# Layer 3 of a graph network with edges on partitions, more selected blocks, and another engine for one kind of transfer

## The chip, the cores and the metric

The kernel runs on one core of a Trainium2 chip. The metric is the time of one execution on the device in microseconds; the figure for a kernel is the median of several runs. A core has TensorE (matmuls and weight loads), VectorE, ScalarE, GpSimd and SyncE; the last three issue DMA transfers too.

## The reference

12,500 nodes with 32 features, 200,000 edges from a node `src` to a node `dst`, sorted by `dst`. Every edge gets a message from a four-layer network, the messages are averaged by `dst`, added to `x`, and each row is normalised.

```python
x_j, x_i = x[src], x[dst]
msg = concatenate([x_i, x_j - x_i], axis=-1)      # (200000, 64)
h = relu(msg @ W1 + b1)                           # 64
h = relu(h @ W2 + b2)                             # 128
h = relu(h @ W3 + b3)                             # 64
m = h @ W4 + b4                                   # 32
s   = segment_sum(m, dst, 12500)
cnt = segment_sum(ones, dst, 12500)
out = layernorm(x + s / maximum(cnt, 1)[:, None])
```

## The kernel before, in words

**Layer 1 is split.** `msg @ W1` is `x_j @ W1b + x_i @ (W1a - W1b)`. A prologue computes for every node the row `z_rows` (source part, f32) and the row `y_rows` (destination part, as three bf16 parts), and stores both in HBM. **Layer 4 is applied after the sum**, since it is linear: the main loop sums `h` of layer 3 and a column of ones by node, into `sums` (65 x 12,584 f32).

**Steps.** The edges are cut into S_N = 196 blocks of 1024 edges, one to a step. A block has two units (h = 0, 1) of 512 edges; a unit has four tiles of 128. The activations of layers 1 to 3 lie with features on partitions and 512 edges in the free dimension. There are two kinds of block:

- *Gathered* blocks (144 of them): GpSimd fetches the source rows with one indirect DMA for each 128 edges (L585, eight a block, 1147 in all, of which the first 40 read `x` itself), into a ring `xj` of R = 10 blocks. GpSimd waits for a ring slot until TensorE has transposed the block that was in it. TensorE turns the rows with four transposes (L919) straight into the PSUM bank of layer 1.
- *Selected* blocks (SB = 52, the first 53,248 edges, which the prologue sorts by source within each block): no gather. VectorE builds one-hots of the sources (L1377, eight chunks a block) and TensorE picks the rows with 113 small bf16 matmuls (L964). These are spread over the block's own step and the two before it (`PIECES`: chunks 0 to 2, then 3 to 5, then 6 and 7). ScalarE and VectorE copy the result (L698, L1386), and six bf16 matmuls apply layer 1 (L978).

`SORTED_AT` spreads the selected blocks evenly over the steps 7 to 188, at least three steps apart. The first AHEAD = 4 steps run in the prologue, between the stages of the sort; the rest is a loop whose number of passes is computed from the data (one pass here).

**One step s on TensorE**, in order: the source rows of s (L919, or the last piece of L964); the destination rows of s, a one-hot `pick` times a window of `y_rows` (L901); the transposes of layer 3 of block s-2 (L1004); the window sum of block s-3, 8 matmuls of `h3t` (128 edges x 65) with the one-hot of the destinations (L1019 gathered, L1016 selected); the pieces of L964 of the coming selected blocks; L978 if s is selected; layer 3 of s-1 (L996, two matmuls of 512 columns with w3s as weights, onto two halves of the partitions); layer 2 of s (L988, likewise on two halves of the rows).

**ScalarE** in step s: relu2 of s-1 (L724, two), copy_x, relu1 of s (L716), relu3 of s-1 (L731). **VectorE**: copy_x, copy_layer3 of s-2 (L1392, PSUM to `h3t`), `build_pick` of s+1 (L1366, L1367, L1369), `build_onehot` of s-2 (L1410, eight), `add_sums` of s-3 (L1425, one addition to `sums` for a selected block, two for a gathered one, with a register read of the window's place before each), then `build_hot` for selected blocks up to three steps on.

**SyncE** issues the block transfers, RX = 3 steps ahead: the dst list (`load_dst`, L458), the window of `y_rows` (`load_rows`, L468 or twice L473, each with a register read of its place), and the source windows of the selected blocks (L491). `load_rows` of s+3 waits until layer 1 of s has read its buffer.

**The tail.** After the last window sum: messages (L1082), transposes (L1092), the mean, the residual and the normalisation in chunks, and the stores.

Of the kernel before, what the change touches and what calls it, by code (L numbers as in the profile page):

```python
# [15 lines left out]
O = 32  # L16
# [15 lines left out]
SB = 52  # L32
# [81 lines left out]
def build(nc, x, src, dst, W1, b1, W2, b2, W3, b3, W4, b4, consts, bounds, out):  # L114
# [3 lines left out]
    with ctx:  # L118
# [44 lines left out]
        b3s = sb("b3s", [P, 1], F32)  # L163

# [56 lines left out]
        h3 = part(work, 8 * UE, (2, UE))  # L221
# [75 lines left out]
        s_l3, s_ht, s_agg = sem("layer3"), sem("layer3_turned"), sem("window_summed")  # L297
        s_h3a = sem("layer3_copied_by_scalar")
# [3 lines left out]
        s_r1, s_r3 = sem("relu1"), sem("relu3")  # L302
# [4 lines left out]
        s_open = sem("pass_open")  # L307
        s_begun = sem("gathers_begun")
# [74 lines left out]
        def _(sp):  # L383
# [34 lines left out]
            sp.dma_start(w3s[:, :], W3).then_inc(s_w, 16)  # L418
            sp.dma_start(b2s[:, :], b2.rearrange("(n a) -> n a", a=1)).then_inc(s_w, 16)
# [41 lines left out]
            def load_rows(s):  # L461
                u = s % RX
                if s >= RX:
                    for h in range(2):
                        sp.wait_ge(s_l1[h], s - RX + 1)
                if is_sorted(s):
                    first = sp.value_load(base_i[0:1, base_at(s, 0):base_at(s, 0) + 1], min_val=0, max_val=N)
                    sp.dma_start(ywin[:, u, :, :], y_rows[bass.ds(first, WIN), :, :].rearrange(  # L468
                        "(k n) c f -> (n c) k f", k=2)).then_inc(s_ywin[u], 16)
                else:  # L470
                    for h in range(2):
                        first = sp.value_load(base_i[0:1, base_at(s, h):base_at(s, h) + 1], min_val=0, max_val=N)
                        sp.dma_start(ywin[:, u, h, :], y_rows[bass.ds(first, KN), :, :].rearrange("n c f -> (n c) f"))\  # L473
                            .then_inc(s_ywin[u], 16)

# [18 lines left out]
            def load_first():  # L494
                for s in range(RX):
                    load_dst(s)
                    load_rows(s)

            def step(s):
# [4 lines left out]
                if s + RX < S_N:  # L504
                    load_dst(s + RX)
                    load_rows(s + RX)
# [11 lines left out]
            sp.wait_ge(s_ypad, 16)  # L518
            rows_stored(sp, s_yst)
# [110 lines left out]
        def _(act):  # L630
# [53 lines left out]
            act.wait_ge(s_w, 15 * 16)  # L684
            act.wait_ge(s_set, 2)

# [31 lines left out]
            def relu2(s):  # L718
                v = s % 2
                for h in range(2):  # L720
                    act.wait_ge(s_l2[h], s + 1)
                    if s >= 2:
                        act.wait_ge(s_l3, 2 * (s - 1))
                    nc.scalar.activation(h2[:, v, h, :], p_h2[:, h, :], ACT.Relu, bias=b2s[:, 0:1]).then_inc(s_r2[h], 1)  # L724

            def relu3(s):
                v = s % 2
                act.wait_ge(s_l3, 2 * (s + 1))
                if s >= 2:
                    act.wait_ge(s_ht, s - 1)  # L730
                nc.scalar.activation(h3[:, v, :], p_h3, ACT.Relu, bias=b3s[:, 0:1]).then_inc(s_r3, 1)  # L731

            def copy_layer3(s):
                act.wait_ge(s_ht, s + 1)
                if s >= 2:
                    act.wait_ge(s_agg, s - 1)
                nc.scalar.activation(h3t[:, s % 2, :, :, 0:H3], p_ht.rearrange("p (t h f) -> p t h f", t=UT, h=2), ACT.Copy)\
                    .then_inc(s_h3a, 1)

            def step(s):  # L740
# [826 lines left out]
```

## Time and profile before

| | |
|---|---|
| median of 3 runs | 1571.46 us (1568.09 to 1571.53) |
| span of the profiled execution | 2441.1 us (no other time of it is given) |
| TensorE matmuls / weight loads busy | 1767.5 us (72%) / 1040.0 us (43%) |
| VectorE busy | 947.9 us (39%) |
| ScalarE busy | 602.6 us (25%) |
| GpSimd busy | 1125.9 us (46%) |
| mean granted TensorE clock | 0.764 of 2.4 GHz |

The profiled execution took 870 us longer than the median run. A share of its span is therefore not a share of an ordinary run: it has to be asked of each stretch whether it looks as it would without the profiler. "Releaser" in the views is what ended an idle time; "issue" means that nothing which the profile shows did.

### The profile page before, as it was taken

Reading aid. Unit: us, or ns where it says so; the run is one execution under the profiler, and the core shown is the slowest. Engines: PE = TensorE matmul, PEld = TensorE weight load, DVE = VectorE, ACT = ScalarE, POOL = GpSimd, SP = SyncE. Lnnn points to the kernel's source line nnn. Section 1 sums busy time; section 2 is a strip of 40 time slices with the busy share of each in tenths; the row PEclk is TensorE's granted clock in tenths of the full one; section 3 lists DMA queues with packets and bytes.
Section 4 is the critical chain, followed back from the end, with each engine's and each line's share of the span. In section 5 each row is a group of like instructions: output and inputs, shape, how many; then the busy total and the mean of one; then the engine's idle time right before and its main releaser. Section 6 shows DMA issues by size and latency. Waiting matters only on the chain.

```text
span 2441.1 us, 39243 instructions
## 1 busy us (share of the span) xinstructions
PE 1767.5 (72%) x13131; PEld 1040.0 (43%) x13131; DVE 947.9 (39%) x3086; ACT 602.6 (25%) x945; POOL 1125.9 (46%) x1165
## 2 busy tenths in 40 slices
PE   3133777777768777878787778786867778777797
PEld 2112444444444444444444444444444444444454
DVE  3663343333333343333333333443333333333356
ACT  2233122222212222212222222222221222122234
POOL 5275444453544454354545454544444454444411
PEclk7555787877878787777778877777877877787888
DMA  5334643343434443353434353544344344444332
GB/s 128 98 93 88 200 112 112 106 140 94 136 101 116 126 121 109 103 147 91 135 105 136 104 152 92 152 109 114 104 123 115 111 114 109 133 118 118 109 106 59
DMA packets 189929, 283.06 MB, mean 116 GB/s; under 512 B 84614, under 2 KB 90169, under 8 KB 189156
## 3 DMA queue, kind: packets, MB, share of 16 engines
q1 hardware_dynamic: 152341, 241.67, 33.7%
q0 software_dynamic: 36704, 37.00, 7.3%
q10 hardware_dynamic: 682, 1.85, 0.3%
q8 instruction: 108, 1.77, 0.3%
q14 instruction: 94, 0.77, 0.1%
HBM read 266.51 MB, written 13.73 MB: 115 GB/s over the span
## 4 chain that ended last, share of the span: by engine, by line
PE 63%; issue 23%; another core or an unknown queue 6%; DVE 3%; ACT 2%; DMA 1%; SPq 1%; DVEq 0%; POOL 0%; ACTq 0%; POOLq 0%
PE ps L964 22%; PE ps L996 12%; PE ps L988 10%; PE ps L1019 5%; PE ps L1004 4%; PE ps L919 3%; PE ps L901 3%; PE ps L1016 2%; PE ps L978 2%; ACT work L716 1%; ACT work L731 1%; DMA sums<-in_src 1%; DVE region L1410 0%; DVE region L1292 0%
## 5 line engine op out<-in xcount | busy, mean ns | idle before, releaser
L585 POOL DMA_INDIRECT xj<-z_rows,src_t x1107 | 1074.5, 971 | 1190.9 <-PE ps L919 787.7
L964 PE MATMUL ps<-region,x_p 128*96 128x150 bf16 (+53 forms) x5876 | 569.6, 243 | 416.6 <-issue 407.2
L964 PEld LDWEIGHTS ps<-region,x_p 128*96 128x96 bf16 x5876 | 440.6, 142 | 572.9 <-issue 566.7
L731 ACT ACTIVATE work<-ps,b3s 128x512 f32<-128x512 f32 x196 | 134.7, 687 | 1335.5 <-PE ps L996 1037.1
L996 PE MATMUL ps<-work,w3s 128*64 128x512 f32 x784 | 356.6, 840 | 21.2 <-issue 21.1
L1377 DVE TENSOR_SCALAR region<-region,cst 128x1565 bf16<-128x1565 int16 (+6 forms) x416 | 245.7, 634 | 268.0 <-remote 256.3
L988 PE MATMUL ps<-work,w2s 64*128 64x512 f32 x784 | 298.1, 827 | 6.8 <-ACT work L716 5.6
L724 ACT ACTIVATE work<-ps,b2s 128x512 f32<-128x512 f32 x392 | 250.7, 684 | 161.0 <-PE ps L988 82.7
L1392 DVE COPY work<-ps 128x512 f32<-128x512 f32 x194 | 133.4, 687 | 336.4 <-PE ps L1004 217.0
L1386 DVE CAST work<-ps 96x512 bf16<-96x512 f32 x52 | 35.7, 686 | 513.9 <-PE ps L964 506.8
L1410 DVE TENSOR_SCALAR region<-iota_g,dst_rel 128x42 f32<-128x42 f32 x1120 | 185.7, 250 | 0.0
L716 ACT ACTIVATE work<-ps,b1s 128x512 f32<-128x512 f32 x196 | 134.8, 688 | 199.9 <-PE ps L901 155.0
L988 PEld LDWEIGHTS ps<-work,w2s 64*128 64x128 f32 x784 | 81.7, 240 | 237.5 <-issue 184.7
L1425 DVE TENSOR_TENSOR sums<-sums,ps 65x42 f32 (+1 forms) x340 | 67.8, 199 | 273.0 <-remote 109.5
L1019 PE MATMUL ps<-region,work 128*65 128x42 f32 x2304 | 168.8, 238 | 5.6 <-DVE sums L1425 3.6
L1019 PEld LDWEIGHTS ps<-region,work 128*65 128x65 f32 x2304 | 166.6, 148 | 8.3 <-issue 8.0
L1004 PE MATMUL ps<-cst,work 128*128 128x128 f32 x784 | 132.9, 294 | 50.1 <-ACT work L731 44.0
L919 PEld LDWEIGHTS ps<-cst,xj 128*128 128x128 f32 x576 | 65.7, 150 | 146.6 <-issue 146.5
L996 PEld LDWEIGHTS ps<-work,w3s 128*64 128x64 f32 x784 | 74.2, 166 | 118.6 <-issue 102.0
L1004 PEld LDWEIGHTS ps<-cst,work 128*128 128x128 f32 x784 | 86.4, 146 | 87.8 <-ACT work L731 54.1
L919 PE MATMUL ps<-cst,xj 128*128 128x128 f32 x576 | 102.1, 304 | 14.3 <-DVE work L1333 14.3
L901 PE MATMUL ps<-region,ywin 126*64 126x512 bf16 x496 | 92.9, 406 | 12.1 <-remote 12.1
(156 smaller groups left out, 826.3 us busy)
## 6 DMA issues: line engine op xcount, KB each, us to landing
dstb<-dst_rows SPq DMA_DIRECT2D x196, 252.0 KB
region<-src_rows SPq DMA_DIRECT2D x104, 391.2 KB
region<-src_rows SPq DMA_DIRECT2D x52, 407.2 KB
region<-src_rows SPq DMA_DIRECT2D x52, 403.2 KB
region<-src_rows SPq DMA_DIRECT2D x52, 376.2 KB
region<-src_rows SPq DMA_DIRECT2D x52, 375.8 KB
region<-src_rows SPq DMA_DIRECT2D x52, 374.0 KB
region<-src_rows SPq DMA_DIRECT2D x52, 366.2 KB
```

The costliest lines, as they stand in the source:

```text
L585: pool.indirect_dma_start(out=xj[:, u, j % UT, j // UT, 0:w], out_offset=None, in_=rows, in_offset=bass.IndirectOffsetOnAxis(ap=cols[:, j: ...
L716: nc.scalar.activation(h1[:, v, :], p_h1, ACT.Relu, bias=b1s[:, 0:1]).then_inc(s_r1, 1)
L724: nc.scalar.activation(h2[:, v, h, :], p_h2[:, h, :], ACT.Relu, bias=b2s[:, 0:1]).then_inc(s_r2[h], 1)
L901: added = nc.tensor.matmul(p_h1[h * H1:(h + 1) * H1, :], rows, pick[:, v, k, h * UE:(h + 1) * UE], start=False, stop=k == steps - 1, skip_ ...
L919: turned = nc.tensor.matmul(to[:, t * T:(t + 1) * T], xj[:, u, t, :, :].rearrange("p h f -> p (h f)"), ident, start=t == 0, stop=True, is_ ...
L964: chosen = nc.tensor.matmul(ps[0:XP, XBANK[h], lo - h * UE:hi - h * UE], xb[:, a, :], hot[:, q % QN, at + lo:at + hi], start=not begun[h], ...
L988: nc.tensor.matmul(p_h2[:, h, :], w2s[r:r + H1, :], h1[r:r + H1, s % 2, :], start=True, stop=True).then_inc(s_l2[h], 1)
L996: nc.tensor.matmul(p_h3[h * H3:(h + 1) * H3, :], w3s[:, :], h2[:, s % 2, h, :], start=True, stop=True).then_inc(s_l3, 1)
L1004: turned = nc.tensor.transpose(p_ht[:, t * T:(t + 1) * T], h3[:, s % 2, t * T:(t + 1) * T], ident)
L1019: summed = nc.tensor.matmul(p_agg[:, h * KN:(h + 1) * KN], h3t[:, v, t, h, :], onehot[:, v, j, 0:KN], start=t == 0, stop=t == UT - 1)
L1377: nc.vector.tensor_scalar(hot[:, q % QN, 0:CW[c]], spread[:, q % QE, 0:CW[c]], cst[:, C_PID:C_PID + 1], None, ALU.is_equal).then_inc(s_hot, 1)
L1410: last = nc.vector.tensor_scalar(onehot[:, v, j, 0:w], nodes[:, :], dst_rel[:, n * PT + j:n * PT + j + 1], None, ALU.is_equal)
```

## The change

Three edits in one:

1. **Layer 3 with edges on partitions.** The activations h2 of 128 edges become the stationary operand and w3s (128 x 64) the moving one, so that the result has edges on partitions, as the window sum needs it. The four transposes, ScalarE's relu3 and the buffer h3 go. The bias can't be a per-partition scalar now: VectorE takes max(h @ W3, -b3) with a row `floor3` that holds -b3, and the missing b3 is added behind the sum, as a bias b3 @ W4 folded into the last row of w4s. The window sum comes one step earlier (block s-2 in step s), layer 3 has two PSUM banks, and the loop has one step fewer at its end. In VectorE's step the copy and `add_sums` stand first, and `build_onehot` is of s-1.
2. **SB = 60.** 60 blocks are selected and 136 gathered, in 1083 indirect DMAs in place of 1147. The selected ones stand three steps apart in 55 of 59 cases, four in the others; before it was 23 of 51.
3. **`load_rows` on ScalarE**, behind relu1 of the step, in place of SyncE. In the prologue ScalarE issues the first three blocks' rows before its step 0.

```diff
-SB = 52
+SB = 60
...
-        p_x, p_h1, p_h3 = ps[:, 0, :], ps[:, 1, :], ps[:, 4, :]
+        p_x, p_h1 = ps[:, 0, :], ps[:, 1, :]
...
-        p_ht = ps[:, 5, :]
+        p_h3 = ps[:, 4:6, :].rearrange("p v (t h f) -> p v t h f", t=UT, h=2)
+        p_b4 = ps[H3:H3 + 1, 7, 256:256 + O]
...
         def layer3_copied(eng, s):
-            if s < AHEAD - 2:
-                eng.wait_ge(s_h3a, s + 1)
-            else:
-                eng.wait_ge(s_h3c, s + 3 - AHEAD)
+            eng.wait_ge(s_h3c, s + 1)
...
+            sp.dma_start(floor3[:, :], b3.unsqueeze(0).to_broadcast([P, H3])).then_inc(s_w, 16)
...
+            act.wait_ge(s_base, 1)
+            act.wait_ge(s_ypad, 16)
+            rows_stored(act, s_yst)
+            load_first_rows()
...
                 if s < S_N:
                     relu1(s)
-                if 2 <= s < AHEAD:
-                    copy_layer3(s - 2)
-                if s >= 1:
-                    relu3(s - 1)
+                if s + RX < S_N:
+                    load_rows(s + RX)
...
             def layer3(s):
-                if s >= 1:
-                    pe.wait_ge(s_r3, s)
+                if s >= 2:
+                    layer3_copied(pe, s - 2)
                 for h in range(2):
                     pe.wait_ge(s_r2[h], s + 1)
-                    nc.tensor.matmul(p_h3[h * H3:(h + 1) * H3, :], w3s[:, :], h2[:, s % 2, h, :],
-                                     start=True, stop=True).then_inc(s_l3, 1)
-            def turn_layer3(s):
-                pe.wait_ge(s_r3, s + 1)
-                if s >= 1:
-                    layer3_copied(pe, s - 1)
-                for t in range(UT):
-                    turned = nc.tensor.transpose(p_ht[:, t * T:(t + 1) * T], h3[:, s % 2, t * T:(t + 1) * T], ident)
-                turned.then_inc(s_ht, 1)
+                    for t in range(UT):
+                        made = nc.tensor.matmul(p_h3[:, s % 2, t, h, :], h2[:, s % 2, h, t * T:(t + 1) * T], w3s[:, :],
+                                                start=True, stop=True)
+                made.then_inc(s_l3, 1)
...
-                stay_busy({S_N + 1: 3}.get(s, 0))
-                if 2 <= s <= S_N + 1:
-                    turn_layer3(s - 2)
-                stay_busy({S_N: 4, S_N + 1: 2, S_N + 2: 8}.get(s, 0))
-                if s >= 3:
-                    sum_window(s - 3)
+                stay_busy({S_N: 4, S_N + 1: 6}.get(s, 0))
+                if s >= 2:
+                    sum_window(s - 2)
...
+            pe.wait_ge(s_w, 16 * 16)
+            nc.tensor.matmul(p_b4, b3s[0:H3, :], w4s[0:H3, :], start=True, stop=True).then_inc(s_b4, 1)
...
+            def last_weights():
+                dve.wait_ge(s_b4, 1)
+                link(nc.vector.tensor_tensor(w4s[H3:H3 + 1, :], w4s[H3:H3 + 1, :], p_b4, ALU.add))
...
             def copy_layer3(s):
-                dve.wait_ge(s_ht, s + 1)
+                dve.wait_ge(s_l3, s + 1)
...
-                nc.vector.tensor_copy(h3t[:, s % 2, :, :, 0:H3], p_ht.rearrange("p (t h f) -> p t h f", t=UT, h=2))\
+                nc.vector.tensor_tensor(h3t[:, s % 2, :, :, 0:H3], p_h3[:, s % 2, :, :, :],
+                                        floor3[:, :].unsqueeze(1).unsqueeze(1).to_broadcast([P, UT, 2, H3]), ALU.max)\
                     .then_inc(s_h3c, 1)
...
             def step(s):
+                if 2 <= s <= S_N + 1:
+                    copy_layer3(s - 2)
+                if s >= 3:
+                    add_sums(s - 3)
                 if s < S_N and is_sorted(s):
                     copy_x(s)
-                if AHEAD <= s <= S_N + 1:
-                    copy_layer3(s - 2)
                 if s + 1 < S_N:
                     build_pick(s + 1)
-                if 2 <= s <= S_N + 1:
-                    build_onehot(s - 2)
-                if s >= 3:
-                    add_sums(s - 3)
+                if 1 <= s <= S_N:
+                    build_onehot(s - 1)
```

## Rows read from the trace of the kernel before

**Rows 1.** The page, its first line.
```profile
span 2441.1 us, 39243 instructions
```

**Rows 2.** The waits: who waited for whom, us in total, times, longest.
```profile
POOL xj L585 <- PE ps L919: 787.7, 101, 14.0
PEld ps L964 <- issue: 566.7, 725, 3.1
```

**Rows 3.** Timeline of TensorE while gathers run: start, us, engine, line, operation, count.
```profile
1006.89 1.71 PE L964 MATMUL ps<-region,x_p 128*96 128x155 bf16 x31
1008.99 0.30 PE L964 MATMUL ps<-region,x_p 128*96 128x148 bf16 x2 [0.40 <-issue]
```

**Rows 4.** Timeline of TensorE after the last gather.
```profile
2353.76 1.09 PE L1019 MATMUL ps<-region,work 128*65 128x42 f32 x16
2354.67 2.41 PE L964 MATMUL ps<-region,x_p 128*96 128x26 bf16 x39
...
2361.66 2.69 PE L964 MATMUL ps<-region,x_p 128*96 128x155 bf16 x45
...
2372.59 0.66 PE L919 MATMUL ps<-cst,xj 128*128 128x128 f32 x4
...
2373.51 0.66 PE L1004 MATMUL ps<-cst,work 128*128 128x128 f32 x4
...
2376.03 1.13 PE L988 MATMUL ps<-work,w2s 64*128 64x512 f32 x4
2377.09 0.66 PE L919 MATMUL ps<-cst,xj 128*128 128x128 f32 x4
```

**Rows 5.** GpSimd: its group of gathers in the page, and four of its timeline.
```profile
L585 POOL DMA_INDIRECT xj<-z_rows,src_t x1107 | 1074.5, 971 | 1190.9 <-PE ps L919 787.7
...
115.66 1.06 POOL L585 DMA_INDIRECT xj<-z_rows,src_t  x1 [43.15 <-DMA z_rows<-work]
...
205.44 0.94 POOL L585 DMA_INDIRECT xj<-z_rows,src_t  x1 [14.89 <-issue]
206.69 0.94 POOL L585 DMA_INDIRECT xj<-z_rows,src_t  x1 [0.30 <-issue]
...
2336.93 0.94 POOL L585 DMA_INDIRECT xj<-z_rows,src_t  x1 [0.30 <-issue]
```

**Rows 6.** Three steps, busy us of PE, PEld, DVE, ACT, POOL; granted clock, DMA.
```profile
2352.34:2372.59 20.25, 20.25 (x221) 13.95 (x220) 13.15 (x46) 8.17 (x13) 0.00 (x0) 1.00 0.13 36
```

**Rows 7.** Weight loads: timeline, and by line (duration ns min/median/max).
```profile
2351.28 0.30 PEld L988 LDWEIGHTS ps<-work,w2s 64*128 64x128 f32 x4 [0.81 <-issue]
...
2353.26 0.42 PEld L1004 LDWEIGHTS ps<-cst,work 128*128 128x128 f32 x4 [0.23 <-issue]
...
L1004 PEld LDWEIGHTS ps<-cst,work x784: 137/141/231, 157.0 to 2411.2; 128*128 128x128 f32 x196
...
L988 PEld LDWEIGHTS ps<-work,w2s x784: 182/187/336, 128.0 to 2404.7; 64*128 64x128 f32 x196
```

**Rows 8.** VectorE's copy and second addition, and SyncE's loads of a gathered block's rows.
```profile
2349.45 0.69 DVE L1392 COPY work<-ps 128x512 f32<-128x512 f32 x1 [2.08 <-PE ps L1004]
...
2352.60 0.20 DVE L1425 TENSOR_TENSOR sums<-sums,ps 65x42 f32 x1 [0.75 <-DVE sums L1425]
...
2354.32 1.69 SPq L473 DMA_DIRECT2D ywin<-y_rows  x2
```

**Rows 9.** The loop's start (VectorE, TensorE), the last step's start, the last window sum.
```profile
206.66 6.81 DVE L1350 TENSOR_SCALAR region<-src,blk 52x26 int16<-52x26 int16 x41
...
230.09 0.26 DVE L1350 TENSOR_SCALAR region<-src,blk 52x155 int16<-52x155 int16 x1 [1.13 <-issue]
...
255.12 0.66 PE L919 MATMUL ps<-cst,xj 128*128 128x128 f32 x4
...
2400.11 0.66 PE L919 MATMUL ps<-cst,xj 128*128 128x128 f32 x4
...
2414.97 1.11 PE L1019 MATMUL ps<-region,work 128*65 128x42 f32 x16 [0.30 <-DVE sums L1425]
```

More of the change, by code:

```diff
@@ L163, in build @@
         b3s = sb("b3s", [P, 1], F32)
+        floor3 = sb("floor3", [P, H3], F32)
         ring_at = 4 * PT * WIN + 4 * PE2
@@ L220, in build @@
         x16 = part(work[:, :].bitcast(BF16), 12 * UE, (2, UE))
-        h3 = part(work, 8 * UE, (2, UE))
         h3t = part(work, 10 * UE, (2, PT * (H3 + 1))).rearrange("p v (t h f) -> p v t h f", t=UT, h=2)
@@ L301, in build @@
         s_moved, s_centre = sem("windows_moved"), sem("centring_chain")
-        s_r1, s_r3 = sem("relu1"), sem("relu3")
+        s_r1 = sem("relu1")
         s_r2 = [sem(f"relu2_unit{n}") for n in range(2)]
@@ L307, in build @@
         s_open = sem("pass_open")
+        s_b4 = sem("bias_through_w4")
         s_begun = sem("gathers_begun")
@@ L459, in load_dst @@
                     .then_inc(s_dwin[u], 16)
[L461 to L474, printed above, removed]
             def store_windows(c):
@@ L496, in load_first @@
                     load_dst(s)
-                    load_rows(s)
             def step(s):
@@ L683, in _, with load_rows, load_first_rows @@
                 split_more(g)
-            act.wait_ge(s_w, 15 * 16)
+            act.wait_ge(s_w, 16 * 16)
             act.wait_ge(s_set, 2)
+            def load_rows(s):
+                u = s % RX
+                if s >= RX:
+                    for h in range(2):
+                        act.wait_ge(s_l1[h], s - RX + 1)
+                if is_sorted(s):
+                    first = act.value_load(base_i[0:1, base_at(s, 0):base_at(s, 0) + 1], min_val=0, max_val=N)
+                    act.dma_start(ywin[:, u, :, :], y_rows[bass.ds(first, WIN), :, :].rearrange(
+                        "(k n) c f -> (n c) k f", k=2)).then_inc(s_ywin[u], 16)
+                else:
+                    for h in range(2):
+                        first = act.value_load(base_i[0:1, base_at(s, h):base_at(s, h) + 1], min_val=0, max_val=N)
+                        act.dma_start(ywin[:, u, h, :], y_rows[bass.ds(first, KN), :, :].rearrange("n c f -> (n c) f"))\
+                            .then_inc(s_ywin[u], 16)
+            def load_first_rows():
+                for s in range(RX):
+                    load_rows(s)
+            act.wait_ge(s_base, 1)
+            act.wait_ge(s_ypad, 16)
+            rows_stored(act, s_yst)
+            load_first_rows()
             def window_sources(c):
@@ L722, in relu2 @@
                     if s >= 2:
-                        act.wait_ge(s_l3, 2 * (s - 1))
+                        act.wait_ge(s_l3, s - 1)
                     nc.scalar.activation(h2[:, v, h, :], p_h2[:, h, :], ACT.Relu, bias=b2s[:, 0:1]).then_inc(s_r2[h], 1)
[L726 to L738, printed above, removed]
             def step(s):
@@ L783, in _ @@
                     act.sem_inc(s_begun, 1)
+                    act.wait_ge(s_tables, 1)
+                    load_first_rows()
                     for s in range(AHEAD):
@@ L1064, in _ @@
                 turn_masked()
-                for s in range(AHEAD, S_N + 3):
+                for s in range(AHEAD, S_N + 2):
                     step(s)
@@ L1179, in weights @@
             def weights():
-                dve.wait_ge(s_w, 15 * 16)
+                dve.wait_ge(s_w, 16 * 16)
                 w = w1par[0:XP, :]
@@ L1464, in _ @@
             count_passes()
+            last_weights()
             dve.wait_ge(s_end, 1)
```

11 lines of the change are left out of this document (5 added, 6 removed).

## The prediction

> **What bounds the kernel now.** I read the page first, then the waits, TensorE's timeline with gathers running and without, GpSimd's rows, and last the weight loads. The profiled execution has a span of 2441.1 us and the median run takes 1571.46, so the profile slowed this kernel by 870 us [rows 1]; no other time of that execution is given, so its span is its own time. The sum can't be made on that span; I first rebuild the median from stretches that show no stall.
>
> The reader should see where the 870 us lie. TensorE's weight loads waited 566.7 us before the small matmuls of L964 to "issue", that is to nothing the program asked for [rows 2]. The timeline shows the form: 31 matmuls of L964 in 1.71 us, then one or two every 0.7 us [rows 3]. Once GpSimd's last gather has started at 2336.93, the same line runs 39 matmuls in 2.41 us and 45 in 2.69 without a gap, at a granted clock of 1.00, the 2.4 GHz level [rows 4, 5, 6]. I take the dribble for a cost of profiling and price TensorE from the clean stretch [rows 4]: a gathered step runs from L919 to L919, 2372.59 to 2377.09, 4.50 us. Two gathered steps and one selected take 2352.34 to 2372.59, 20.25 us with TensorE busy for all of it [rows 6], so a selected step is 20.25 - 9.0 = 11.25.
>
> Two accounts of the median follow. TensorE: step 6 starts at 255.12 and step 195 at 2400.11, the end of the span is 41 us later [rows 9]. Before step 6 VectorE's 59 copies of L1350 ran at 6.81 us for 41, to 213.5, and then dribbled too, the other 18 until 230.4; at the first pace those take 3.0 us, so I start at 255 - 14 = 241 [rows 9]. 241 + 137 x 4.50 + 52 x 11.25 + 41 = 1484. GpSimd: gathers from z_rows begin at 115.66, and there are 1107 of them; undisturbed ones start 1.25 us apart, and the mean is 0.971 busy + 0.30 = 1.27; the wait for the pass count costs 14.6 more than such a gap; after the last gather comes at least the last step with its tail, 41 [rows 5, 9]. That gives 115.7 + 1107 x 1.25 to 1.27 + 14.6 + 41 = 1555 to 1577. The median lies inside this second account and 87 us above the first. So unprofiled the gathers set the pace, though in the profiled execution GpSimd waited 787.7 us for TensorE [rows 2]: there it was TensorE that was held up.
>
> **The change part by part.**
>
> *60 blocks instead of 52.* 64 of 1147 gathers go: 64 x 1.27 = 81 us off GpSimd. TensorE swaps 8 gathered for 8 selected steps: 8 x (11.25 - 4.50) = +54 us. VectorE gets 8 x 8 source one-hots of about 0.6 us and is busy 13.15 of the 20.25 us of three steps now [rows 6], so this hides. Selected steps stand 3 apart nearly everywhere (55 of 59 distances; before 23 of 51).
>
> *Layer 3, removed.* Four transposes (L1004), the window sum (L1019) and both 512-column matmuls of L996 take from 2373.51 to L988 at 2376.03 in a gathered step: 2.52 us, of which the sum comes back in another place [rows 4]. ScalarE's relu of 0.69 us goes too; it is not on the path, since ScalarE is busy 8.17 of 20.25 [rows 6].
>
> *Layer 3, added.* Eight matmuls with 128 edges as the stationary side and 64 moving columns. An f32 matmul leaves two records (16 for the eight of L1019 [rows 4]), so that is 16 weight loads of 128 f32 columns. No row shows a full-height one in a dense stream; the bounds come from its neighbours. Low: L1019 loads 65 columns and reaches the next line 0.91 us later, 57 ns a record [rows 4]. Next: the transposes of L1004 load 128 columns, but four in 0.42 us with 0.14 each, so (0.42 - 0.14) / 3 = 94 ns [rows 7]. Nearest: L988 loads 128 f32 columns per row half, two at once; four take 0.30 and each 0.187, so the second pair follows after 0.11 us [rows 7]. High: load and stream not overlapped, L988's 0.107 and a stream like L1019's whole record of 0.057, 0.16. I take the load's own time, 0.107, and the 2 ns that a stream adds where it never stops (L1019's 57 against 54, two cycles for each of 65 columns at 2.4 GHz, the rate that also makes 107 out of 128): 0.109 us. 16 x 0.109 = 1.75, plus 0.91 for the window sum (its value when a full-width line follows) and 0.10 for the change to L988's half tiles, as now before it. 2.76 against 2.52: +0.24 us per step, although fewer columns are streamed. 189 steps: +45 us.
>
> The rule that speaks against this change is in the Trainium skill, TensorE: Matmul & The Clock Gate, section LDWEIGHTS: a load takes its columns divided by 1.2 ns, whatever the rows. It gives 107 ns for 128 columns and the trace's 0.11 us agrees; for 96 columns of bf16 it gives 80, and L964's 39 matmuls in 2.41 us (62 ns each, loads included) [rows 4] disagree. By the page alone layer 3 is 16 x 107 = 1.71 us; by the rows 1.75.
>
> *Waits inside the step.* VectorE now copies layer 3 of s-2 first in step s, as a maximum from the same bank; L1392 took 0.69 [rows 8], and the maximum has the same 512 columns, so 0.69 (no row shows its two-operand form). Then it adds the sums: two additions, 0.94 us start to start [rows 8]. Layer 3 of s-2 ends 1.06 us before TensorE's step s begins, and the copy starts about 0.15 later, so the copy ends at -0.2 and the second addition at +0.9. TensorE wants both at +0.92 (L919 to L1004, 2372.59 to 2373.51 [rows 4]). No stall while VectorE is on time. In a selected step it also has copy_x, pick, one-hot and three source one-hots ahead of the next copy: by these rows it ends about 0.3 us late, 60 x 0.25 = 15 us at most. I take 7.
>
> *ScalarE issues the dst rows.* Two loads with their register reads took SyncE 1.69 us a gathered step [rows 8]. ScalarE goes from 0.69 x 4 to 0.69 x 3 + 1.69 = 3.8 us in a step of 4.74. They are issued behind relu1, for buffers that layer 1 of the same step has just freed, so they wait for nothing; queued behind them is relu2, which waits for L988 anyway, ending at about +4.9 when they are over at +3.8. Cost 0. Without that cover it is up to 1.1 us a step. SyncE's queue loses the loads and keeps its dst lists and windows; GpSimd's is untouched. In the prologue six loads (5 us) stand before step 0, beside the sort on VectorE: I take 0, with 5 as the bound.
>
> *Rest.* The bias matmul and five tiny operations of VectorE before the loop: +1.5 us. One step fewer at the end saves a window sum of 1.11 and the additions behind it, 0.94: -2 [rows 8, 9].
>
> **The sum.** TensorE: 241 + 129 x 4.74 + 60 x 11.49 + 41 + 1.5 - 2 = 1582, + 7 for VectorE = 1589. GpSimd: 1571 - 81 = 1490. The longer decides: the bound moves from the gathers to TensorE, and 1589 is 1.1% above the median. About 0.3% (5 us) is what a measurement here can tell from no change.
>
> **Rivals.** Each ns of the load pace is worth 189 x 16 = 3.0 us. No change (1566 to 1576) lies at 101 to 105 ns.
>
> 1. *The loads are cheaper, and the gathers stay the bound* (the other side). If full-height loads follow each other as L1019's do, TensorE needs 1589 - 3.0 x 52 = 1433, and GpSimd's 1490 decides; at the transposes' 94 ns it is 1589 - 45 = 1544. The point from which it is faster: under 101 ns. For it: both paces stand in the trace. Against it: the first has half the columns, the other transposed data; L988's second pair waited the full 0.11.
> The same page of the Trainium skill (Back-to-back issue gap) gives 81 ns for a sustained pair of load and 128-column matmul. Here that would be 1589 - 84 = 1505, by a stream that hides the load better than L988 shows; L964's 62 ns are below it, for bf16.
>
> 2. *TensorE was the bound already*, with 87 us of stalls that the clean stretch doesn't show, some of the "issue" being real. Then nothing comes back from the gathers: 1571 + 54 + 45 - 1 = 1669. For it: the stalls in [rows 3]. Against it: the gather account meets the median with no free term.
>
> 3. *VectorE or ScalarE gets late*, as copies and additions now stand at the head of VectorE's step: 0.2 to 0.3 us on each of 189 steps, 1625 to 1645.
>
> 4. *The change does not do what it says*: what it takes from the gathers and what it lays on TensorE cancel, 1566 to 1576; at 101 to 105 ns.
>
> **How the numbers follow.** Forecast (TensorE bound, 1576 to 1615) 0.40; rival 1 0.30 (0.20 near 1490 to 1505, 0.10 at 1520 to 1560); rival 2 0.13; rival 3 0.07; rival 4 0.10. Faster 0.30, same 0.10, slower 0.60. The likeliest case's own range is 1576 to 1615. From 1490 to 1645 leaves out rival 2 and a few in a hundred of the low end; both signs lie in it.
>
> **What would show it.** In the clean stretch after the last gather: 16 loads of layer 3 in about 1.8 us (at 0.9 rival 1, at 2.6 no overlap); a gathered step of about 4.7; L1019 or L1016 without a wait on VectorE; relu2 starting just behind L988 (else ScalarE's issues delay it). GpSimd's undisturbed pace still 1.25, with 1083 gathers. The prediction is wrong if that step is under 4.5 us, or if the median sits on GpSimd's account, near 1490.

## The result and the profile after

The changed kernel takes 1607.61 us (median of 4 runs, 1604.63 to 1611.45) against 1569.83 for the kernel before on the same chip: a ratio of 1.0251, 95% interval 1.0224 to 1.0278. It is slower by more than twice what was forecast (1589 us, +1.2% on this median). Its profiled execution was one of these runs (1604.63 us, span 1602.7), so this profile, unlike the one of before, can be read as an ordinary run.

The page of the changed kernel: the span; the chain of work that ended last, by line; then two groups (count | busy us, mean ns | idle before).

```profile
span 1602.7 us, 43751 instructions
...
POOL xj L565 73%; DMA sums<-in_src 1%; PE ps L987 0%; PE ps L1003 0%; PE ps L1065 0%; DVE region L1280 0%; DVE region L1279 0%; DVE work L1140 0%; DMA xj<-z_rows,src_t 0%; PE ps L840 0%; DMA z_rows<-work 0%; DVE work L1146 0%; PE ps L1075 0%; PE ps L978 0%; POOL region L597 0%
...
L565 POOL DMA_INDIRECT xj<-z_rows,src_t x1043 | 1162.4, 1114 | 317.9 <-issue 317.3
```

The chain is gathers for 73% of the span: GpSimd is still the bound. 1043 gathers from z_rows (1107 before, [rows 5]) take 1114 ns each, plus 0.305 idle (317.9 / 1043): 1.419 us start to start, where the prediction had 1.27. Undisturbed ones are as short as ever, 0.94 us. The two timelines show where the rest lies, first GpSimd's, then VectorE's.

```profile
299.64 0.94 POOL L565 DMA_INDIRECT xj<-z_rows,src_t  x1 [0.30 <-issue]
300.89 0.95 POOL L565 DMA_INDIRECT xj<-z_rows,src_t  x1 [0.30 <-issue]
302.14 2.83 POOL L565 DMA_INDIRECT xj<-z_rows,src_t  x1 [0.30 <-issue]
305.28 0.95 POOL L565 DMA_INDIRECT xj<-z_rows,src_t  x1 [0.30 <-issue]
...
1019.75 0.94 POOL L565 DMA_INDIRECT xj<-z_rows,src_t  x1 [0.30 <-issue]
1020.99 0.95 POOL L565 DMA_INDIRECT xj<-z_rows,src_t  x1 [0.30 <-issue]
1556.64 0.94 POOL L565 DMA_INDIRECT xj<-z_rows,src_t  x1 [0.30 <-issue]
```

```profile
301.27 1.29 DVE L1401 TENSOR_SCALAR region<-iota_g,dst_rel 128x42 f32<-128x42 f32 x8
302.48 1.69 DVE L1365 TENSOR_SCALAR region<-region,cst 128x1629 bf16<-128x1629 int16 x3
304.29 0.69 DVE L1382 TENSOR_TENSOR work<-ps,floor 128x512 f32<-128x512 f32 x1
...
1019.95 1.67 DVE L1365 TENSOR_SCALAR region<-region,cst 128x1565 bf16<-128x1565 int16 x3
```

The gather of 302.14 lasts 2.83 us, and VectorE builds three source one-hots (L1365) under it, from 302.48 to 304.17; it ends 0.80 us behind them. Yet the row of three that begins at 1019.95 costs nothing. From 280 to 1500 us the gathers last 157 us more than 0.944 each would make, and all but 12 of these 157 lie on gathers that overlap such one-hots. A row of three that begins 0.32 to 0.34 us behind a gather's start holds it up for 1.87 to 1.89 us (31 rows, 58 us together), one that begins 0.20 or 0.21 behind it for none (41 rows).

TensorE, two gathered steps and one selected in the middle of the run, and its transposes near the end:

```profile
1010.35 1.71 PE L954 MATMUL ps<-region,x_p 128*96 128x144 bf16 x29
...
1017.21 0.66 PE L909 MATMUL ps<-cst,xj 128*128 128x128 f32 x4
1017.80 0.41 PE L891 MATMUL ps<-region,ywin 126*64 126x512 bf16 x2
1018.34 1.11 PE L1003 MATMUL ps<-region,work 128*65 128x42 f32 x16
1019.28 2.41 PE L954 MATMUL ps<-region,x_p 128*96 128x26 bf16 x39
1021.53 1.94 PE L987 MATMUL ps<-w3s,work 128*128 128x64 f32 x16
1023.40 1.13 PE L978 MATMUL ps<-work,w2s 64*128 64x512 f32 x4
...
1032.22 0.99 PE L954 MATMUL ps<-region,x_p 128*96 128x144 bf16 x13
...
1521.07 1.09 PE L909 MATMUL ps<-cst,xj 128*128 128x128 f32 x4 [5.89 <-DMA xj<-z_rows,src_t]
```

It runs nearly without a gap until about 1500 us, three steps in 21.87 us (1010.35 to 1032.22), and waits for gathers only in the last blocks: 5.89, 1.33, 5.89 and 1.10 us, 14.2 together. Until then it lives on the blocks that GpSimd had fetched ahead. Behind the second of the long waits the granted clock is 0.50 (1545 to 1557 us), the lower of its two levels (1.2 GHz), and the sixteen matmuls of L987 take 3.66 us in place of 1.98, so that the waits cost more than the 14.2. So two accounts end close to each other again, GpSimd's at 1603 and TensorE's some 20 us below.

### The profile page after: what moved, and what is told of

Read it like the earlier page. It is cut to its first block, busy times and chain, and to the rows that moved or that the text cites. A ratio compares the mean times of both kernels' runs of the same rounds, so it can differ in the third digit from the quotient of the medians.

```text
span 1602.7 us, 43751 instructions
## 1 busy us (share of the span) xinstructions
PE 1456.2 (91%) x15630; PEld 1161.9 (72%) x15630; DVE 993.4 (62%) x3162; ACT 468.7 (29%) x755; POOL 1219.8 (76%) x1101
## 4 chain that ended last, share of the span: by engine, by line
POOL 73%; issue 20%; PE 2%; DVE 2%; DMA 1%; ACT 0%; DVEq 0%; SPq 0%; POOLq 0%; ACTq 0%
POOL xj L565 73%; DMA sums<-in_src 1%; PE ps L987 0%; PE ps L1003 0%; PE ps L1065 0%; DVE region L1280 0%; DVE region L1279 0%; DVE work L1140 0%; DMA xj<-z_rows,src_t 0%; PE ps L840 0%; DMA z_rows<-work 0%; DVE work L1146 0%; PE ps L1075 0%; PE ps L978 0%; POOL region L597 0%
## 5 line engine op out<-in xcount | busy, mean ns | idle before, releaser
L565 POOL DMA_INDIRECT xj<-z_rows,src_t x1043 | 1162.4, 1114 | 317.9 <-issue 317.3
L954 PEld LDWEIGHTS ps<-region,x_p 128*96 128x96 bf16 x6780 | 389.2, 124 | 45.5 <-issue 45.5
L954 PE MATMUL ps<-region,x_p 128*96 128x127 bf16 (+54 forms) x6780 | 409.5, 218 | 0.0
L987 PE MATMUL ps<-w3s,work 128*128 128x64 f32 x3136 | 394.6, 280 | 0.0
L987 PEld LDWEIGHTS ps<-w3s,work 128*128 128x128 f32 x3136 | 375.9, 196 | 25.1 <-issue 25.1
L1382 DVE TENSOR_TENSOR work<-ps,floor 128x512 f32<-128x512 f32 x196 | 135.4, 691 | 320.8 <-PE ps L987 316.4
L1365 DVE TENSOR_SCALAR region<-region,cst 128x1629 bf16<-128x1629 int16 x480 | 272.3, 617 | 8.4 <-DMA region<-src_rows 7.3
L978 PE MATMUL ps<-work,w2s 64*128 64x512 f32 x784 | 227.9, 659 | 0.9 <-ACT work L720 0.9
L1003 PE MATMUL ps<-region,work 128*65 128x42 f32 x2176 | 157.3, 236 | 23.8 <-DVE sums L1416 9.4
L1003 PEld LDWEIGHTS ps<-region,work 128*65 128x65 f32 x2176 | 144.4, 143 | 45.4 <-issue 37.7
L1000 PEld LDWEIGHTS ps<-region,work 128*65 128x65 f32 x960 | 73.5, 139 | 28.0 <-issue 28.0
L1000 PE MATMUL ps<-region,work 128*65 128x84 f32 x960 | 81.9, 239 | 11.8 <-DVE sums L1416 6.0
L1401 DVE TENSOR_SCALAR region<-iota_s,dst_rel 128x84 f32<-128x84 f32 x480 | 89.7, 277 | 0.0
```

Of the source, the lines that this page charges most:

```text
L565: pool.indirect_dma_start(out=xj[:, u, j % UT, j // UT, 0:w], out_offset=None, in_=rows, in_offset=bass.IndirectOffsetOnAxis(ap=cols[:, j: ...
L954: chosen = nc.tensor.matmul(ps[0:XP, XBANK[h], lo - h * UE:hi - h * UE], xb[:, a, :], hot[:, q % QN, at + lo:at + hi], start=not begun[h], ...
L978: nc.tensor.matmul(p_h2[:, h, :], w2s[r:r + H1, :], h1[r:r + H1, s % 2, :], start=True, stop=True).then_inc(s_l2[h], 1)
L987: made = nc.tensor.matmul(p_h3[:, s % 2, t, h, :], h2[:, s % 2, h, t * T:(t + 1) * T], w3s[:, :], start=True, stop=True)
L1000: summed = nc.tensor.matmul(p_agg, h3t[:, v, t, h, :], onehot[:, v, j, :], start=j == 0, stop=j == PT - 1)
L1003: summed = nc.tensor.matmul(p_agg[:, h * KN:(h + 1) * KN], h3t[:, v, t, h, :], onehot[:, v, j, 0:KN], start=t == 0, stop=t == UT - 1)
```

## The experiments

Two theories and a third. **G**: GpSimd's gathers set the end in both kernels, and VectorE's one-hots hold gathers up, more in the changed one. **T**: TensorE sets the end of the changed kernel; long gathers are a by-product. **D**: transfers or their queues stretch the gathers. "Ratio" is to the kernel before, with the 95% interval.

### One part at a time

**e1**, loads of the dst rows on ScalarE, all else as before. 

> The kernel before with edit 3 alone: ScalarE issues the dst rows. Theory G (GpSimd's gathers set the pace in both kernels; in the changed one VectorE's work stretches a gather from 1.25 to 1.41 us start to start): no change, 1565 to 1575 us, and a gather at its old mean. Rival D (the loads on ScalarE's queue are what stretches the gathers): 0.14 us on each of 1107 gathers, 1600 us or more. Rival T (TensorE is what the changed kernel waits for): no change. If the profile of this one is not slowed by the profiler, it also shows which engine the old schedule waits for.

**e2**, `SB = 60` in place of 52, all else as before. 

> The kernel before with edit 2 alone: SB = 60. Theory G: 64 gathers fewer take 80 us off GpSimd, the stretch of 8 more selected blocks gives 10 to 25 back, and TensorE's account of 1484 + 54 = 1538 is close: 1530 to 1550 us. Rival T in its strong form (TensorE was the bound already, rival 2 of the prediction): 1571 + 54 = 1625. Rival D: as G.

**e3**, the new layer 3 and VectorE's new order, all else as before. 

> The kernel before with edit 1 alone: the new layer 3 with VectorE's new order, SB = 52, loads on SyncE. Theory G, with the stretch as a result of VectorE's new order: about 3 us for each of 52 selected blocks where it was 1, so 1107 gathers at 1.39 us, 1660 to 1680 us. Rival T: TensorE 1484 + 45 = 1529, hidden under the gathers: 1565 to 1580. If the stretch is there in the old order too, also 1565 to 1580.

**e4**, the changed kernel with the old layer 3. 

> The changed kernel with its edit 1 undone (old layer 3, SB = 60, loads on ScalarE). Theory G: as SB = 60 alone, 1530 to 1550 us. Rival D: 1600 or more. Rival T: TensorE's 1538, so 1535 to 1545, and then layer 3 is worth 60 to 70 us in the changed kernel instead of the 45 of the prediction.

Measured: e1 1568.31 us, ratio 1.0004 (0.9994 to 1.0014); e2 1566.38, 0.9993 (0.9977 to 1.0010); e3 1632.87, 1.0432 (1.0408 to 1.0456); e4 1554.08, 0.9911 (0.9894 to 0.9928). The loads are free in the kernel before, as forecast. With SB = 60 they are worth 12 us: e2 and e4 differ in them alone. Eight more selected blocks alone are worth nothing, where G had expected 20 to 40 us. The new layer 3 costs 65 us alone and 53 in the full change. Only e1 fell into G's range; e3 lies 27 us below it and e4 4 us above, so G's direction held and the size of the hold-up was not forecast. The groups of gathers in the four pages, in this order:

```profile
L566 POOL DMA_INDIRECT xj<-z_rows,src_t x1107 | 1106.0, 999 | 337.5 <-issue 336.2
```

```profile
L585 POOL DMA_INDIRECT xj<-z_rows,src_t x1043 | 1126.0, 1080 | 317.9 <-issue 317.0
```

```profile
L584 POOL DMA_INDIRECT xj<-z_rows,src_t x1107 | 1162.8, 1050 | 337.5 <-issue 335.6
```

```profile
L566 POOL DMA_INDIRECT xj<-z_rows,src_t x1043 | 1110.2, 1064 | 317.9 <-issue 317.0
```

Same instruction, same program on GpSimd, and its mean runs from 999 to 1114 ns. In none of them does GpSimd wait for TensorE for longer than the 0.3 us that it pauses anyway. So its account can be written down: e1's span of 1565.9 us less 1107 x (0.999 + 0.305) = 1443.5 leaves 122 for what lies ahead of the first gather (78) and behind the last (44). With 122 + gathers x (mean + 0.305):

| kernel | gathers | mean us | account | span |
|---|---|---|---|---|
| e2, SB = 60 | 1043 | 1.080 | 1567 | 1565.7 |
| e3, new layer 3 | 1107 | 1.050 | 1622 | 1626.6 |
| e4, old layer 3, SB = 60 | 1043 | 1.064 | 1550 | 1552.3 |
| the change | 1043 | 1.114 | 1602 | 1602.7 |

All four spans are met within 5 us. Each mean is that of the same profile, so the account shows that the time follows the gathers' length, and not why that differs. In e2 the 64 gathers that go save 83 us, and 0.081 us on each of the other 1043 takes 84 back; a row of three one-hots costs 0.14 us in e1 and 0.82 in e2 (280 to 1500 us). D falls with e1 and e4: the loads on ScalarE's queue make no gather longer (1.064 us in e4, 1.080 in e2 with the loads on SyncE). The other transfers are tested by e5. T is not refuted by these, since TensorE's account is close too.

### The one-hots taken away

**e5** cuts every source one-hot to 64 columns, in the changed kernel; **e6** does so in e3, **e16** in the kernel before.

```diff
-                nc.vector.tensor_scalar(hot[:, q % QN, 0:CW[c]], spread[:, q % QE, 0:CW[c]], cst[:, C_PID:C_PID + 1], None,
+                if q < QN:
+                    nc.vector.memset(hot[:, q, :], 0.0).then_inc(s_hot, 1)
+                    return
+                w = 64
+                nc.vector.tensor_scalar(hot[:, q % QN, 0:w], spread[:, q % QE, 0:w], cst[:, C_PID:C_PID + 1], None,
```

> The changed kernel, but each of VectorE's source one-hots (480, 0.62 us each) covers 64 columns in place of up to 1629; the first five are set to zero instead. So the rows of the selected blocks are wrong. Semaphores, transfers and TensorE's work are those of the changed kernel. Theory G (the gathers set the end, and they are long because VectorE's one-hots hold them up): every gather at 0.94 us busy, 1.25 start to start; GpSimd's account falls to 78 + 1043 x 1.25 + 14 + 45 = 1441 us, and the time to TensorE's own account, 1575 to 1590 us; GpSimd then waits for TensorE in the profile. Rival T (TensorE sets 1607 and long gathers are a by-product): 1603 to 1611. Rival D (transfers stretch the gathers): gathers stay at 1.41 us, 1603 to 1611.

> The same shortening of the one-hots in the kernel with the new layer 3 alone (SB = 52, loads on SyncE, 1632.9 us as it is). Theory G: gathers at 1.25 us, GpSimd's account 123 + 1107 x 1.25 = 1507 us, TensorE's by the prediction 1529: 1525 to 1540 us, about 100 less. Rival T (layer 3 is dear on TensorE itself, some 60 us): 1615 to 1633. Rival D: 1630.

> The kernel before with the source one-hots cut to 64 columns (the rows of the selected blocks are wrong; TensorE's work, transfers and semaphores stay). Theory G: the gathers pay 0.035 us less each than the 0.999 of the kernel with loads on ScalarE, 123 + 1107 x 1.265 = 1523, TensorE's 1484 below it: 1515 to 1530 us. If TensorE had been the bound before (rival 2 of the prediction): 1560 to 1570.

Measured: e5 1581.09 us, ratio 1.0107 (1.0085 to 1.0129); e6 1533.58, 0.9805 (0.9780 to 0.9831); e16 1527.78, 0.9749 (0.9724 to 0.9775). All three lie inside G's ranges, 27, 99 and 41 us below the same kernels with full one-hots. From e5's page, and its waits (engine and line waited for: us, times, longest):

```profile
L565 POOL DMA_INDIRECT xj<-z_rows,src_t x1043 | 1002.8, 961 | 394.1 <-issue 303.9
...
POOL xj L565 <- PE ps L909: 90.3, 46, 2.6
```

The gathers are back at 0.961 us, and now GpSimd waits for TensorE, 90.3 us in 46 places, which it never did in the changed kernel. TensorE did the same matmuls in both, at the same pace: three steps take 21.89 us in e5 (1001.31 to 1023.20). T had 1603 to 1611 and falls. D falls altogether, since the transfers are the same. Layer 2 of step 188 and of step 195 show where the time goes, in the changed kernel and then in e5:

```profile
1509.03 1.13 PE L978 MATMUL ps<-work,w2s 64*128 64x512 f32 x4
...
1569.28 1.13 PE L978 MATMUL ps<-work,w2s 64*128 64x512 f32 x4
```

```profile
1506.90 1.13 PE L978 MATMUL ps<-work,w2s 64*128 64x512 f32 x4
...
1544.36 1.13 PE L978 MATMUL ps<-work,w2s 64*128 64x512 f32 x4
```

Up to step 188 TensorE is 2 us apart in the two; the last seven steps take 60.2 us in the one and 37.5 in the other, since in the changed kernel they wait for gathers and then run at a lower clock. Nor is it VectorE's lateness: TensorE waits 9.4 and 6.0 us for `add_sums` in the changed kernel (L1003, L1000) and 12.3 and 4.5 in e5.

The runs also split the price of the new layer 3 at SB = 52: with the one-hots cut it costs 6 us (e6 less e16), with them whole 65 (e3). So some 59 of the 65 are hold-ups.

e16's mean is 0.963 with 1107 gathers: 122 + 1107 x 1.268 = 1526, its span 1525.8. So before the change, too, GpSimd was the bound.

### The same one-hots in another order

**e7**, the changed kernel, and **e8**, the old layer 3 with SB = 56: one-hots one at a time between VectorE's other work.

```diff
+                todo = [(STEPS[s + lead], c) for lead in (1, 2, 3) if s >= AHEAD and s + lead < S_N and is_sorted(s + lead)
+                        for c in PIECES[3 - lead]]
...
                 if s >= 3:
                     add_sums(s - 3)
+                if todo:
+                    build_hot(*todo.pop(0))
...
                 if s + 1 < S_N:
                     build_pick(s + 1)
+                if todo:
+                    build_hot(*todo.pop(0))
```

> The changed kernel with the same work in another order on VectorE: the two or three source one-hots of a step no longer stand in a row at its end (1.7 us together), but one behind add_sums, one behind build_pick, the rest behind build_onehot. Theory G: one of 0.6 us can hold a gather up for less than a row of three (up to 1.9 us): stretch of a gather from 0.17 to 0.05 to 0.10 us on the mean, and the time to 1580 to 1590, TensorE's account. Rival T: 1603 to 1611, or more, since VectorE's copies and picks come later. If the stretch goes by the total of one-hot time and not by how it lies, no change in it.

> Old layer 3, SB = 56, loads on ScalarE, the source one-hots spread: one behind build_pick, one behind build_onehot, the rest behind add_sums. Theory G: TensorE's account 1484 + 4 x 6.75 = 1511; GpSimd's 123 + 1075 x 1.25 = 1467 plus a stretch of 0.03 to 0.08 us a gather, 1500 to 1553; so 1511 to 1550, best of all so far. Rival T: about 1540 to 1560, between the kernel before and the one with SB = 60.

Measured: e7 1580.86 us, ratio 1.0101 (1.0078 to 1.0123), as e5; e8 1608.30, 1.0277 (1.0255 to 1.0299), where G had 1511 to 1550. The gathers of e7, then e8:

```profile
L565 POOL DMA_INDIRECT xj<-z_rows,src_t x1043 | 1068.1, 1024 | 330.8 <-issue 311.4
```

```profile
L566 POOL DMA_INDIRECT xj<-z_rows,src_t x1075 | 1164.2, 1083 | 327.7 <-issue 326.8
```

With e7 TensorE is the bound again, and G's range of 1580 to 1590 is met. e8 still meets the account (122 + 1075 x 1.388 = 1614, span 1615.6), so GpSimd's price is right and only the size of the hold-up was guessed wrong. One at a time, a one-hot of 0.63 us costs 0.16 us in e7 and 0.31 in e8 (from 280 to 1500 us). Spreading them is no remedy that can be relied on: the cost goes by where they fall in the gather's 1.25 us, and that changes with every schedule.

### The mode of the one-hot

The Trainium skill has two rules that bear on this. SBUF — State Buffer, Who interferes with whom: GpSimd reaches SBUF through VectorE's second pair of ports, and a VectorE instruction in a mode that uses both pairs, if it comes first, blocks GpSimd, descriptor writing included, until it is over. Vector Engine (DVE) Microarchitecture Reference, Performance modes: a one-source instruction on 16-bit data takes the four-a-cycle mode only if the outermost dimensions of input and output are both even, or equal; otherwise it runs at two a cycle on one pair. No run here sees a port; what follows tests the rule's consequence.

**e9** to **e11** gave the output rows. 

> The changed kernel with each source one-hot written to an output of 3, 5, 7 or 11 rows (same addresses, same values; the chunk of 1613 columns gets two columns more) while the input stays one run. The Trainium skill (Vector Engine (DVE) Microarchitecture Reference, Performance modes) says that a one-source instruction then leaves the four-wide mode that holds both port pairs and runs at two elements a cycle on one pair; SBUF - State Buffer says that only the two-pair modes hold GpSimd up. Theory G with this mechanism: a one-hot takes about 0.9 us in place of 0.62, the gathers stay at 0.94 us all the same, and the time falls to TensorE's 1580 to 1590 although VectorE works 130 us more. Rival: the hold-up comes from VectorE's long instructions whatever their mode: gathers as long as before or longer, 1600 to 1640 us. If the one-hot stays at 0.62 us, the shape did nothing and the run says nothing.

> Old layer 3, SB = 60, loads on ScalarE (1554 us), with the one-hots written in rows. Theory G: GpSimd's account 123 + 1043 x 1.25 = 1427, TensorE's 1484 + 54 = 1538: 1535 to 1545 us. Rival (mode does not matter): 1555 to 1600.

> The same with SB = 54, where the two accounts meet: GpSimd 123 + 1091 x 1.25 = 1487, TensorE 1484 + 2 x 6.75 = 1498. Theory G: 1495 to 1510 us, 4% under the kernel before. Rival (mode does not matter): 1555 to 1600.

Measured: e9 1611.41 us, ratio 1.0273 (1.0236 to 1.0310); e10 1550.23, 0.9895 (0.9865 to 0.9924); e11 1561.29, 0.9971 (0.9955 to 0.9987). In e9's page the one-hot still takes 616 ns:

```profile
L1369 DVE TENSOR_SCALAR region<-region,cst 128x1629 bf16<-128x1629 int16 x480 | 271.9, 616 | 8.4 <-DMA region<-src_rows 7.3
```

Rows without a gap are one run in memory, and were probably merged back to one; that is not shown, since a view gives only the number of columns. The expectation had said that a one-hot of 0.62 us would make the run say nothing, and so it is: G's three ranges are missed, and these runs say nothing on the mode. e9 and e10 repeat the changed kernel and e4. e11 is a point at SB = 54, with the account at 122 + 1091 x 1.317 = 1559 and the span 1558.3:

```profile
L568 POOL DMA_INDIRECT xj<-z_rows,src_t x1091 | 1104.6, 1012 | 332.6 <-issue 330.5
```

**e12** (the changed kernel) and **e13**, **e15** (old layer 3, loads on ScalarE, SB = 54 and 56) put a column of padding between the rows of the input, written so by the transfer:

```diff
+CX = [w + -w % 3 for w in CW[:-1]] + CW[-1:]
+ROWS = [3] * (CN - 1) + [5]
...
+        def padded(q, c):
+            r, w = ROWS[c], CX[c] // ROWS[c]
+            return spread[:, q % QE, 0:r * (w + 1)].rearrange("p (r w) -> p r w", r=r)[:, :, 0:w]
...
-                nc.vector.tensor_scalar(hot[:, q % QN, 0:CW[c]], spread[:, q % QE, 0:CW[c]], cst[:, C_PID:C_PID + 1], None,
+                to = hot[:, q % QN, 0:CX[c]].rearrange("p (r w) -> p r w", r=ROWS[c])
+                nc.vector.tensor_scalar(to, padded(q, c), cst[:, C_PID:C_PID + 1], None,
```

> The changed kernel, with the source windows written by their transfer as 3 (the last chunk 5) rows with one column of padding between them, so that the input of a one-hot really has three rows where its output is one run; same values, up to two columns more. Theory G with the mechanism of the Trainium skill (Vector Engine (DVE) Microarchitecture Reference, Performance modes; SBUF - State Buffer, Who interferes with whom): the one-hot goes from 0.62 to about 0.9 us and no longer holds GpSimd: gathers at 0.94 to 0.97 us, time 1578 to 1590 us, TensorE's account. Rival (long instructions hold the gathers up in any mode): gathers 1.12 us or more, 1607 to 1640 us. If the three times as many packets of the windows make them late, VectorE or TensorE waits for them and the time rises above 1590 with short gathers.

> Old layer 3, SB = 54, loads on ScalarE, windows in padded rows. Theory G: GpSimd 123 + 1091 x 1.25 = 1487, TensorE 1484 + 13.5 = 1498: 1495 to 1512 us. Rival: gathers stay at 1.01 us or more, 1555 to 1570.

Measured: e13 1510.25 us, ratio 0.9640 (0.9607 to 0.9673), inside G's range; e12 1626.08, 1.0380 (1.0344 to 1.0416), outside all but the last clause. From e12's page and waits:

```profile
L573 POOL DMA_INDIRECT xj<-z_rows,src_t x1043 | 1004.8, 963 | 436.3 <-issue 302.1
...
L1375 DVE TENSOR_SCALAR region<-region,cst 128x1629 bf16<-128x1629 int16 x480 | 459.4, 1006 | 7.8 <-DMA region<-src_rows 7.5
...
POOL xj L573 <- PE ps L917: 134.2, 52, 3.2
...
PE ps L1011 <- DVE sums L1426: 58.6, 64, 4.4
```

From e13's timelines, three one-hots and the gathers across them:

```profile
1003.89 2.86 DVE L1396 TENSOR_SCALAR region<-region,cst 128x1566 bf16<-128x1566 int16 x3
...
1002.83 0.95 POOL L574 DMA_INDIRECT xj<-z_rows,src_t  x1 [0.30 <-issue]
1004.08 0.94 POOL L574 DMA_INDIRECT xj<-z_rows,src_t  x1 [0.30 <-issue]
1005.32 0.94 POOL L574 DMA_INDIRECT xj<-z_rows,src_t  x1 [0.30 <-issue]
1006.57 0.94 POOL L574 DMA_INDIRECT xj<-z_rows,src_t  x1 [0.31 <-issue]
```

The one-hots are 60% longer, and no gather is held up by them: of 98 rows of three in e13 between 280 and 1500 us not one adds 0.1 us. The run beside it is e11, with the same split and no padding: gathers of 1.012 us against 0.966, 1561.29 us against 1510.25. That settles length against form: what holds a gather is the fast form of the one-hot, not VectorE's being busy, as the two pages say. GpSimd is still the bound in e13 (122 + 1091 x 1.271 = 1509, the span 1509.4), where G had put TensorE; its account at 1.25 us a gather was too low.

e12 is slow for another reason, the last line of its waits: after 2.86 us of one-hots VectorE comes late to `add_sums`, which now stands at the head of its step, and TensorE waits 58.6 us in 64 places. **e14** spreads the one-hots as e7 does, on top of the padding. 

> The changed kernel with padded windows (1626 us, gathers 0.96, one-hots 1.01 us) and, besides, the one-hots of a step spread: one behind add_sums, one behind build_pick, the rest behind build_onehot. Theory V (the 1626 come from VectorE being late with add_sums after a row of three one-hots of 2.86 us: TensorE waited 0.9 us for it once per selected block): the wait goes, 1578 to 1590 us, TensorE's account. Rival (the three times as many packets of the windows slow TensorE's or VectorE's data): 1615 to 1630.

Measured: 1585.43 us, ratio 1.0119 (1.0093 to 1.0145), inside theory V's range: 41 us of e12's excess were that lateness, and the packets are not at fault.

**e15** moves the balance. 

> Old layer 3, padded windows, loads on ScalarE, SB = 56 in place of 54. GpSimd's account 123 + 1075 x 1.271 = 1489, TensorE's 1484 + 27 = 1511: 1508 to 1520 us, TensorE the bound. If the clean stretch made TensorE's account too long, 1495 to 1505.

Measured: 1501.03 us, ratio 0.9587 (0.9561 to 0.9614), the fastest of all and 4.1% under the kernel before. That is below the 1508 to 1520 expected and in the range of the second case. GpSimd's account is 122 + 1075 x 1.270 = 1487 and the span 1498.3, and the chain that ended last is 79% TensorE, so TensorE is the bound; its forecast of 1511 was 10 too long.

```profile
PE 79%; DVE 5%; issue 5%; ACTq 4%; DMA 4%; ACT 2%; SPq 0%; POOL 0%; DVEq 0%; POOLq 0%
```

## Why the prediction was wrong

The direction was right and the size was not: +2.5% where +1.2% was forecast. The time lies in the range of the likeliest case, 1576 to 1615, by luck: that case had TensorE as the bound and GpSimd at 1490, and it was GpSimd, at 1602. One of the prediction's own signs of being wrong came, a time that sits on GpSimd's account, though not near 1490.

- **GpSimd is the bound before the change.** Right (e16). Its account of 1555 to 1577 came out, but by offsetting terms: gathers begin at 78, not 115.7 us; the 14.6 us of waiting for the pass count isn't on GpSimd in e1's profile; and a gather costs 1.304 from start to start, not 1.25 to 1.27 (e1, whose time is that of the kernel before). The slowed profile had fewer hold-ups than an ordinary run.
- **"GpSimd: 1571 - 81 = 1490", at a pace "still 1.25".** This is the step that failed. Of the undisturbed gather the 1.25 is right. The mean rose from 1.304 to 1.419: the 64 gathers that go save 83 us, and 0.115 on each of the other 1043 costs 120. So 122 + 1043 x 1.419 is 1602. The prediction priced VectorE's source one-hots as VectorE's time only, "so this hides", and never asked what they do to GpSimd; no rival had it. A sign stood in its own rows: a gather of 0.971 us on the mean beside an undisturbed one of 0.94 [rows 5]. In that trace the gathers last 29 us more than 0.944 each would make, and 20 of these lie on gathers that overlap the one-hots.
- **"The bound moves from the gathers to TensorE."** Wrong by 20 us. Without hold-ups it does (e5, e7: GpSimd waits).
- **TensorE: 1582, with 7 for VectorE 1589.** e5 measured 1581 (span 1577.7). The sum is nearly right by terms that cancel. The loop begins earlier than taken: step 6 at 181 us, not 242.5. Three steps take 21.87, not 20.97. The three-step base was itself 20.90, not 20.25 (e4, first part of layer 1 to the next, below), with 0.61 us of idle time before it that the stretch behind the last gather doesn't show.

```profile
1008.06 0.84 PE L987 MATMUL ps<-work,w1p 96*64 96x512 bf16 x6 [0.61 <-issue]
1028.96 0.84 PE L987 MATMUL ps<-work,w1p 96*64 96x512 bf16 x6 [0.63 <-issue]
```

- **Layer 3: +0.24 us per step, +45.** Measured (21.87 - 20.90) / 3 = +0.32 (between e4 and the changed kernel). The sixteen loads take 1.87 us (1021.53 to 1023.40), 0.117 each, not 1.75; none of the lower prices that the prediction weighed came out. (Its 94 ns for the transposes is 93 by its own rows; nothing hangs on it.) Besides, 0.54 us pass from the dst rows to the window sum (1017.80 to 1018.34) where 0.34 was the old distance: the second addition ends at 1018.20, 0.99 after the step's start, not +0.9, and the sum starts 0.14 later. It is late by 0.2 in two steps of three, 24 us, where 7 were taken.
- **Rest, +1.5 us.** Too low by about 9: in the prologue TensorE now waits 7.21 us for VectorE's copy of layer 3, and VectorE begins the 59 copies of the sort's end at 148.09 us instead of 138.37 (e4). In the changed kernel it hid behind the gathers.
- **ScalarE's loads, 0.** Right at SB = 52 (e1); at SB = 60 they gain 12 us (e4 less e2), by shorter hold-ups.
- **Rival 1's loads under 101 ns, rival 2, rival 4's standstill**: none came. Rival 2 had +54 us for SB = 60 alone, and e2 has none. Rival 3 (VectorE late) is real where its one-hots are long (e12), small here.

Layer 3's 53 us in the full change (e4 to the change) are not its loads: GpSimd's account alone gives 1602 - 1550 = 52. On TensorE the new layer 3 costs, by an estimate from the three steps, 0.32 x 189 = 61 us and about 10 in the prologue. At SB = 52 it stays hidden even without hold-ups, since GpSimd's account is about as long (e6: 122 + 1107 x 1.269 = 1527, the span 1532.2); at SB = 60 most of it would show with the hold-ups gone, but no run has the old layer 3 at SB = 60 without them. What stays open is why edit 1 brings the one-hots into the costly part of the gather's 1.25 us so often: rows of two cost 0.91 us each in the changed kernel and 0.22 in e4, rows of three 0.86 and 0.79 (280 to 1500 us). No run separates VectorE's new order from the new matmuls, and no rule for where the rows fall was found: in e4 rows of three that begin 0.15 us behind a gather's start cost up to 1.71.

## What to carry to other kernels

When an engine is the bound by a long train of equal instructions, compare that train's mean with its undisturbed value in an unslowed profile before pricing anything else; the difference is a cost with a cause, and every edit on the neighbouring engine can move it. A gather issued by GpSimd is held up by VectorE's long one-input work on 16-bit data in its fast form; a shape that gives up this form made VectorE's one-hots 60% longer and the kernel 3% faster at the same split (e11 to e13). Balance the two ways of fetching rows only after that, since fewer gathers for more one-hots can come out at nothing (e2); with the split set anew it is 4.1% under the kernel before (e15).

## What the runs showed of the hardware

- An indirect transfer of 128 rows takes 0.94 us of GpSimd and 0.30 between two. Under a row of three one-hots it took up to 2.84 us in the changed kernel, and this depended on 0.1 us of phase: no hold-up at +0.20, 1.88 us at +0.33 behind the gather's start. Of its 109 gathers over 1.3 us from 280 to 1500 us 94 ended 0.8 us behind the last one-hot and 14 ended 0.1 behind it. The page SBUF — State Buffer of the Trainium skill (A bandwidth-pool intuition that's wrong) gives "~115 ns" from the end of the VectorE instruction for its own probe; the 14 agree, the 94 don't. Its rule that the one that comes second is fully blocked (Who interferes with whom) doesn't give the 41 rows at +0.20 either, which ran beside two gathers with no loss to them and took 1.68 us, as long as the rows that held a gather up.
- The one-hot of up to 1629 int16 columns took 0.62 to 0.66 us on the mean of a kernel as one run and 1.01 with an input of three padded rows; the gathers beside it fell from 1.114 to 0.963 us.
- The loads of 128 f32 columns at full height, each with a matmul of 64 columns, follow each other at 1.87 / 16 = 0.117 us at a granted clock of 1.00.
